# Reordering the passage between attention and experts in a one-core AdaLN block, two gate products first

## The reference

```python
mod = (silu(c) @ wmod).reshape(B, 6, 1, -1)
sa, ca, ga, sb, cb, gb = (mod[:, k] for k in range(6))
ga, gb = sign(ga) * max(|ga|, 0.25), sign(gb) * max(|gb|, 0.25)

h = layernorm(x) * (1 + ca) + sa                 # first half: linear attention, 16 heads of 16
Q, K, V = fm(h @ Wq.T + bq), fm(h @ Wk.T + bk), h @ Wv.T + bv      # fm(t) = elu(t) + 1
KV, Ksum = sum over tokens of K x V per head, sum over tokens of K
out = (Q @ KV) / (Q . Ksum + 1e-6)
x = x + ga * (out @ Wo.T + bo)

h = layernorm(x) * (1 + cb) + sb                 # second half: 8 experts, top 2
logits = cosine(h, centroids) + h @ w_route.T
g = softmax over the two largest logits
x = x + gb * sum_e g_e * (gelu(h @ w1[e] + b1[e]) @ w2[e] + b2[e])
```

## Time and profile before

| | us |
|---|---|
| median of 3 runs (376.76 to 378.42) | 376.76 |
| the profiled execution | 376.92 |
| its span, first to last instruction | 375.2 |
| PE busy, DVE busy | 350.4 (93%), 289.2 (77%) |
| POOL busy, ACT busy | 280.3 (75%), 231.3 (62%) |
| mean granted TensorE clock, share of full | 0.982 |
| DMA moved | 31.68 MB, 84 GB/s |

### The profile page before, as it was taken

How to read it: one execution, slowest core, us unless ns; L and a number is a source line. 1 busy time by engine, 2 the same in 40 slices (tenths; PEclk the granted TensorE clock), 3 DMA queues, 4 the chain that set the end, 5 groups by cost and what they waited for, 6 DMA issues and landing times.

```text
span 375.2 us, 9187 instructions
## 1 busy us (share of the span) xinstructions
PE 350.4 (93%) x2762; PEld 326.4 (87%) x2762; DVE 289.2 (77%) x820; ACT 231.3 (62%) x504; POOL 280.3 (75%) x388
## 2 busy tenths in 40 slices
PE   7999999999988474999999999999999999999895
PEld 6877888888867363999999999999999999999895
DVE  3778777778877797797797787877977977966753
ACT  4385878787745225685674764855756756756541
POOL 3457999999786739789789888888888798677200
PEclk9999999999999958999999999999999999999999
DMA  7943620000000030312214224214214223233221
GB/s 265 331 138 100 209 59 0 0 0 2 1 2 0 2 113 2 114 58 86 100 65 120 85 63 134 85 57 140 78 63 129 73 80 118 83 86 129 85 71 56
DMA packets 23704, 31.68 MB, mean 84 GB/s; under 512 B 2288, under 2 KB 14204, under 8 KB 23680
## 3 DMA queue, kind: packets, MB, share of 16 engines
q1 hardware_dynamic: 23240, 31.34, 26.6%
q10 hardware_dynamic: 440, 0.04, 0.1%
HBM read 27.04 MB, written 4.34 MB: 84 GB/s over the span
## 4 chain that ended last, share of the span: by engine, by line
PE 59%; POOL 7%; DVE 5%; issue 4%; ACT 1%; POOLq 0%; DVEq 0%
PE bank L741 18%; PE bank L743 17%; PE bank L742 17%; PE bank L749 3%; PE bank L917 2%; POOL x_sb L411 1%; PE bank L956 1%; POOL k_sum L404 1%; POOL tr_lo L394 1%; POOL early L441 1%; POOL early L451 1%; POOL rstd L378 1%; PE bank L874 1%; DVE den L1240 1%; DVE early L1213 0%
## 5 line engine op out<-in xcount | busy, mean ns | idle before, releaser
L690 ACT ACTIVATE bank<-bank,cols_sb 128x256 f32<-128x256 f32 x128 | 51.4, 439 | 46.5 <-PE bank L743 46.4
L478 POOL TENSOR_TENSOR hid_pair<-hid_g,hid_pair 128x512 fp32r<-128x512 f32 x56 | 72.5, 1294 | 7.0 <-ACT hid_pair L697 4.6
L741 PE MATMUL bank<-tr_hi,w_hi 128*128 128x256 f32 x256 | 74.2, 290 | 0.0
L743 PE MATMUL bank<-tr_hi,w_lo 128*128 128x256 f32 x256 | 72.6, 283 | 0.0
L742 PE MATMUL bank<-tr_lo,w_hi 128*128 128x256 f32 x256 | 72.4, 283 | 0.0
L741 PE MATMUL bank<-w_hi,hid_pair 128*128 128x256 f32 x252 | 70.2, 278 | 0.0
L743 PE MATMUL bank<-w_hi,hid_pair 128*128 128x256 f32 x252 | 70.1, 278 | 0.0
L742 PE MATMUL bank<-w_lo,hid_pair 128*128 128x256 f32 x252 | 70.1, 278 | 0.0
L697 ACT ACTIVATE hid_pair<-hid_g 128x512 fp32r<-128x512 f32 x64 | 40.4, 632 | 28.7 <-DVE hid_g L1298 27.4
L741 PEld LDWEIGHTS bank<-tr_hi,w_hi 128*128 128x128 f32 x256 | 48.9, 191 | 0.2
L742 PEld LDWEIGHTS bank<-tr_lo,w_hi 128*128 128x128 f32 x256 | 48.9, 191 | 0.1
(11 more groups left out here) (154 smaller groups left out, 916.7 us busy)
## 6 DMA issues: line engine op xcount, KB each, us to landing
g_bc<-g_dram SPq DMA_DIRECT2D x64, 256.0 KB, 3.5
x_sb<-in_x SPq DMA_DIRECT2D x16, 256.0 KB, 3.0
out<-x_sb SPq DMA_DIRECT2D x15, 256.0 KB, 2.3
early<-in_wmod SPq DMA_DIRECT2D x3, 512.0 KB, 7.0
q_sb<-in_w SPq DMA_DIRECT2D x2, 512.0 KB, 6.3
q_sb<-in_w SPq DMA_DIRECT2D x1, 1024.0 KB, 9.4
mod_row<-mod_dram SPq DMA_DIRECT2D x1, 1024.0 KB, 6.0
q_sb<-in_wqkvT SPq DMA_DIRECT2D x2, 384.0 KB, 5.4
```

The lines of the kernel that those rows point to most:

```text
L478: gp.tensor_tensor(hid_lo[:, p, :, :], hid_g[:, p % 2, :, :], hid_hi[:, p, :, :].bitcast(F32), ALU.subtract).then_inc(e_hlo, 1)
L690: last = ac.activation(half, half, ACT.Gelu, bias=b1_sb[:, e:e + 1])
L741: te.matmul(out_ap, l_hi, r_hi, start=start, stop=False, skip_group_check=shared)
L743: return te.matmul(out_ap, l_lo, r_hi, start=False, stop=stop, skip_group_check=shared)
```

## The change

It moves work about in the passage and leaves what is computed as it is.

- Units 13, 14 and 15 (`cast_at_end`): ScalarE makes `tr_hi` (`cast_activations`) and the expert weights' `w_hi` (`cast_weights`) in steps 12 to 14, on semaphores of their own; VectorE only subtracts.
- TensorE: `first(0, 0)` in front of `tp_o(2)`, then `first(0, 1)` to `first(0, 3)` in a row, all in step_e(-1). ScalarE does unit 0's four `gelu` there, between its other pieces.
- `mask_kv` is cut in two. `keep_ksum(1)` stays in step_e(-1); `mask_kv(1)` goes to the end of VectorE's step 0, `make_m(1)` (now in bank 7) in TensorE's step 1 behind `tp_e(3)`, `split_m(1)` to the end of VectorE's step 1. `attend` waits for it from unit 5 on, `normalise_e` (bank 7) from unit 4 on.
- VectorE: `gate(0, 0)` and `gate(0, 1)` at the head of step 0, in front of `gates_a(1)`. `denominators(3)` goes behind `modulate_e(1)`.
- GpSimd: `norm_e(0)` in front of `make_qz(2)`; `make_prod(3)` behind `exp_gates(0)`; `add_bo` of units 12 and 13 at the end of step 0, of units 14 and 15 at the end of step 1.

The diff, cut to its core:

```diff
@@ GpSimd @@
-                wait(pool, a_hi, u.count(1, 1))
+                if cast_at_end(u):
+                    wait(pool, a_hi_end, u.count(1, 1) - (NU - 3))
+                else:
+                    wait(pool, a_hi, u.count(1, 1))
...
                     exp_gates(u.plus(1))
+                if u.nth(-1):
+                    make_prod(u.plus(4))
...
-                if u.nth(-1):
-                    for j in (3, 2, 1):
-                        add_bo(unit(NU - j))
+                if u.nth(0) or u.nth(1):
+                    for j in range(2):
+                        add_bo(unit(NU - 4 + 2 * u.count(1, 0) + j))
...
+            norm_e(u0)
             make_qz(unit(2))
-            make_prod(unit(3))
-            add_bo(unit(NU - 4))
-            norm_e(u0)
@@ ScalarE @@
+            def cast_activations(u):
+                wait(act, a_hf, u.count(1, 1))
+                wait(act, a_v, u.count(1, -1))
+                ac.activation(tr_hi[:, u.h, :, :], tr_f[:, u.h, :, :], ACT.Copy).then_inc(a_hi_end, 1)
+            def cast_weights(u):
+                i = u.count(1, 0)
+                act.wait_ge(d_w, 48)
+                ac.activation(w_hi[:, i, :], w_raw[:, i, :], ACT.Copy).then_inc(w_hi_end, 1)
...
                     modulate(u.plus(1), u.plus(1).batch())
+                if u.plus(1) and cast_at_end(u.plus(1)):
+                    cast_activations(u.plus(1))
...
                     keep_v(u)
+                if u.plus(1) and cast_at_end(u.plus(1)):
+                    cast_weights(u.plus(1))
...
+                if of_later_units(u, 4):
+                    act.wait_ge(f_m_read, B)
...
+                if u.nth(-1):
+                    gelu(u.plus(1), 0)
                 if u.plus(3):
                     hi_o(u.plus(3))
...
+                if u.nth(-1):
+                    gelu(u.plus(1), 1)
                 if u.plus(2):
                     normalise_e(u.plus(2))
+                if u.nth(-1):
+                    gelu(u.plus(1), 2)
+                    gelu(u.plus(1), 3)
@@ TensorE @@
+                if of_later_units(u, 5):
+                    pe.wait_ge(f_ready, B)
                 wait(pe, o_lo, u.count(1, 1))
...
-                if u.nth(0) and p == 2:
-                    pe.wait_ge(f_m_read, B)
+                if u.nth(0) and p == 3:
+                    pe.wait_ge(f_ksrow, B)
...
-                    pe.wait_ge(f_ready, B)
                     pe.wait_ge(b2_ready, 3)
...
+                if u.nth(-1):
+                    first(u.plus(1), 0)
                 if u.plus(3):
                     tp_o(u.plus(3))
...
                 if u.nth(-1):
-                    first(u.plus(1), 0)
+                    for p in range(1, NP):
+                        first(u.plus(1), p)
...
-                if u.nth(-1):
-                    make_m(1, bank[4])
-                    first(u.plus(1), 1)
-                if u:
+                if u and not u.nth(0):
                     first(u, 2)
...
                     tp_e(u.plus(2))
+                if u.nth(1):
+                    make_m(1, bank[7])
@@ VectorE @@
             def step_e(u):
+                if u.nth(0):
+                    gate(u, 0)
+                    gate(u, 1)
                 if u.plus(1):
                     gates_a(u.plus(1))
-                if u.plus(4):
+                if u.nth(-1):
+                    keep_ksum(1, bank[5][:, 0:E])
+                if u.plus(4) and not u.nth(-1):
                     denominators(u.plus(4))
...
-                if u.nth(-1):
-                    mask_kv(1, bank[5][:, 0:E])
...
                     modulate_e(u.plus(2))
+                if u.nth(-1):
+                    denominators(u.plus(4))
                 if u.plus(3):
                     add_attention(u.plus(3))
-                if u.nth(-1):
-                    split_m(1, bank[4])
...
                     lo_e(u.plus(2))
+                if u.nth(0):
+                    mask_kv(1)
+                if u.nth(1):
+                    split_m(1, bank[7])
```

More of the change, by code:

```diff
@@ L211, in adaln_block @@
         b2_split = sem("b2_split"); b2_ready = sem("b2_ready")
-        w_hi_done = sem("w_hi_done"); w_ready = sem("w_ready")
+        w_hi_done = sem("w_hi_done"); w_hi_end = sem("w_hi_end"); w_ready = sem("w_ready")
         a_bo = sem("a_bo")
@@ L216, in adaln_block @@
         a_st = sem("a_st"); a_eps = sem("a_eps"); a_stats = sem("a_stats"); a_pow = sem("a_pow"); a_rstd = sem("a_rstd")
-        a_xn = sem("a_xn"); a_tp = sem("a_tp"); a_hf = sem("a_hf"); a_hi = sem("a_hi"); a_lo = sem("a_lo")
+        a_xn = sem("a_xn"); a_tp = sem("a_tp"); a_hf = sem("a_hf"); a_hi = sem("a_hi"); a_hi_end = sem("a_hi_end"); a_lo = sem("a_lo")
         a_qk = sem("a_qk"); a_v = sem("a_v"); a_exp = sem("a_exp"); a_vs = sem("a_vs"); a_neg = sem("a_neg")
@@ L258, in sums, with cast_at_end, of_later_units @@
             return bank[7 * t][:, 0:E] if u.nth(NU - 1) else bank[6][:, t * E:(t + 1) * E]
+        def cast_at_end(u):
+            return any(u.nth(NU - j) for j in (1, 2, 3))
+        def of_later_units(u, i):
+            return not any(u.nth(j) for j in range(i))
         def kv_bank(u):
@@ L1171, in split_weights @@
                 hi = w_hi[:, bass.ds(i, 1), :]
-                ve.tensor_copy(hi, src).then_inc(w_hi_done, 1)
-                wait(dve, w_hi_done, u.count(1, 1))
+                if cast_at_end(u):
+                    wait(dve, w_hi_end, u.count(1, 1) - (NU - 3))
+                else:
+                    ve.tensor_copy(hi, src).then_inc(w_hi_done, 1)
+                    wait(dve, w_hi_done, u.count(1, 1))
                 TT(w_lo[:, bass.ds(i, 1), :], src, hi.bitcast(F32), ALU.subtract).then_inc(w_ready, 1)
@@ L1180, in step_a @@
                     split_weights(u)
-                if u.plus(1):
+                if u.plus(1) and not cast_at_end(u.plus(1)):
                     split_a(u.plus(1))
@@ L1200, in _, with keep_ksum, mask_kv @@
             pipeline(ve, step_a, 2, 4, NU - 4, NU - 3)
-            def mask_kv(b, sums):
+            def keep_ksum(b, sums):
                 dve.wait_ge(f_ksum, b + 1)
                 ve.tensor_copy(ksum_row[:, b, :], sums).then_inc(f_ksrow, 1)
+            def mask_kv(b):
                 dve.wait_ge(f_ksrow, b + 1)
@@ L1408, in step_e @@
                     lo_e(u.plus(2))
+                if u.nth(0):
+                    mask_kv(1)
+                if u.nth(1):
+                    split_m(1, bank[7])
             dve.wait_ge(mod_got, 16)
             ve.memset(kv_m[:, :, :], 0.0)
-            mask_kv(0, bank[0][:, 0:E])
+            keep_ksum(0, bank[0][:, 0:E])
+            mask_kv(0)
             step_a(unit(NU - 3))
```

## The result

| | before | changed |
|---|---|---|
| median, first measurement (8 executions each) | 377.79 us | 373.81 us |
| lowest to highest | 376.76 to 378.97 | 373.41 to 376.31 |
| ratio, 95% interval | | 0.9913 [0.9892, 0.9933] |
| median, measured again (experiment 9) | 377.86 us | 375.60 us |
| ratio, 95% interval | | 0.9935 [0.9913, 0.9957] |

The change makes the kernel faster by 0.65 to 0.9% by the ratios, which is 2.5 to 3.3 us; the medians differ by 4.0 and 2.3. I had forecast 5.0, and a time of 371.8; the range of 369.8 to 375.0 holds the first median and not the second.

What follows compares the result with a forecast made beforehand. The passage was taken as a chain of VectorE work, with TensorE's backlog setting the end after it. Step 1 6.5 us earlier, - 1.0 - 0.8 + 0.3 = 5.0, gave 371.8 us from 376.76; range 369.8 to 375.0.

Steps and rivals of the forecast that it cites:

- The table load and g_bc: ScalarE's second table load hidden under first(0,0), else 1.3 us later; g_bc delays the gate products 0 to 0.5, taken 0.
- the rival of a late chain: Table load behind gelu's wait, g_bc landing late and blocking VectorE, some half clock: 374.0 us; chance 0.11.
- the one in which half clock lasts into step 1: Slower: TensorE's clock falls at 133.2 and stays at half in steps 0 and 1, up to some 383 us; chance 0.06.
- the signs of being wrong: VectorE idle before gate(0,0), late table load, second(0,3) or attend(5) waiting over 1 us for GpSimd, half-clock step 1, late route(2).
- Casts of units 13 to 15: Before the passage: moving these casts to ScalarE gains between 0 and 1.03 us, taken 0.7.
- second(0,0) with 14 matmuls at half clock 3.1: TensorE, step 0 behind tp_e(2): this block takes 3.1 us at half clock, with route(2) ending at 151.2.
- Here the two products in front cost their whole 1.2 us: VectorE, head of step 0: gate(0,0) and gate(0,1) delay unit 1's gates and attend(3) by 1.2 us.
- Taken 0.8: Steps behind the passage: loss from add_bo on GpSimd and VectorE's added work, bounds 0 and 2.5 us, taken 0.8.
- The +0.3 in my sum: Steady step before: about 0.3 us of stall it held, counted again, so added back to the gain.
- The rival in which GpSimd is late next: GpSimd's 2.5 us lag in steps 0 and 1 falls on TensorE nearly whole: 373.5 us; chance 0.17.
- the one without a gain: Holes only move: VectorE's chain carries 1.2 us more, ScalarE's casts take back 0.7, two rivals added: 376.2 us; chance 0.09.
- TensorE's new waits in attend are met long before: TensorE, attend from unit 5 on: the new waits are already met and cost nothing.

Runs made afterwards that it cites:

- experiment 9: The changed kernel unaltered, measured again against the kernel before: median 375.60 us, ratio 0.9935.
- Experiment 3: Changed kernel with add_bo of units 12 to 15 moved into GpSimd's idle holes: median 372.30 us, ratio 0.9843 to the kernel before.
- experiment 5: Changed kernel with add_bo in GpSimd's holes and mask_kv(1) cut short (units 8 to 15 wrong): 371.91 us, ratio 0.9861 to the kernel before.
- experiment 11: Changed kernel with add_bo in GpSimd's holes and both new waits out of the loop: 373.38 us, ratio 0.9876 to the kernel before.
- experiment 12: Changed kernel with add_bo in GpSimd's holes, TensorE's wait out of the loop, extra matmuls around tp_e(0): 372.07 us, ratio 0.9833 to the kernel before.
- experiment 7: Changed kernel with the casts of units 13 to 15 back on VectorE: 375.62 us, ratio 0.9940 to the kernel before.
- experiment 1: Changed kernel with TensorE's wait in attend and ScalarE's in normalise_e out of the loop: 374.94 us, ratio 0.9919 to the kernel before.
- experiment 10: Changed kernel with 6 and 11 more matmuls around tp_e(0), filling TensorE's holes: 373.97 us, ratio 0.9912 to the kernel before.
- Experiment 6: Changed kernel with gate(0,0) and gate(0,1) back in their steady places in step 0: 376.28 us, ratio 0.9955 to the kernel before.
- experiment 4: Changed kernel with mask_kv(1) cut short (units 8 to 15 wrong), add_bo not moved: 375.64 us, ratio 0.9934 to the kernel before.
- experiment 2: Changed kernel with only TensorE's wait in attend out of the loop, ScalarE's kept: 374.55 us, ratio 0.9912 to the kernel before.
- experiment 8: Changed kernel with 30 more matmuls filling TensorE's hole in front of attend(3): 376.01 us, ratio 0.9941 to the kernel before.

## Why the prediction was right, and where not

**The direction and the chain held.** Step -1 and step 0 are plain work of VectorE in written order: from the end of route(0) to the end of add_attention(3) I had 20.0 us (125.7 to 145.7), measured 19.6 (124.72 to 144.30). The hole in front of attend(3) was forecast at 3.9 with half clock behind it, and is 3.71 with half clock. The table load and g_bc were hidden as said. With that the rival of a late chain did not occur, nor the one in which half clock lasts into step 1: it ended at 143.8, and step 1 began at 148.4. The start of gate(0,0), 135.37, and the end of route(2), near 148.6, came before the times that I had named as signs. Of the signs of being wrong one appeared in part: attend(5) waited 1.30 us, about half of it behind add_bo (0.58 to 0.75 are left in experiments 3, 5, 11 and 12).

**Casts of units 13 to 15: 0.7 was too low, 1.3 by experiment 7.** As far as I had followed the path it was right: counted from `kv` of unit 9, z(0) moved by 0.1 and make_qz(0) by 0.6. What I left out comes behind it: VectorE's w_lo of unit 15, in front of the add_attention that tp_o(1) waits for, took 0.41 instead of 1.17 us.

**"second(0,0) with 14 matmuls at half clock 3.1" failed.** In this profile the clock was back at full during the wait for add_attention(3), and tp_e(2) to route(2) took 3.9 us instead of 5.3. With the casts (0.5 above my 0.7 at route(0)), the 0.4 of the chain and the earlier start of the first half (0.46) that is the 2.8 to 2.9 by which step 1 started sooner than forecast. It was the luck of this execution in part: in the profiles of experiments 1, 3, 10 and 12 half clock lasted beyond tp_e(2), which took 1.09 instead of 0.63, and the second interval was 13.50 to 14.54 instead of 13.42.

**"Here the two products in front cost their whole 1.2 us" failed.** Experiment 6 says the opposite. I had priced them against a VectorE that is never idle, while my own row of times had route(1) over at 137.3, 0.7 behind the end of the work in front. They cost 0.36 there and saved more behind.

**"Taken 0.8" for GpSimd and VectorE behind the passage was the large error.** The four waits are 3.46 us. Experiment 3 takes 2.25 out by moving add_bo alone, and 2.0 to 2.1 by the cleaner comparison; make_m(1), from its start to that of second(1,0), is 0.73, against 1.0. Of the 4.88 given back these two leave 0.7 to 0.8, in which TensorE is busy longer; that is not taken apart. The +0.3 in my sum, for stall in the steady step before, has no row behind it: TensorE was idle for 0.00 us in step 1 and 0.13 in step 2. The rival in which GpSimd is late next was thus the right mechanism, with about its price of 2.5. Two things made it dearer than my hand count. Step 1 started 2.9 us earlier, so mask_kv(1) was no longer under the wait for route(2), as I had said of an early TensorE but at 0.5. And mask_kv(1) took 2.95 instead of 2.3, and split_m(1) 2.83, near the 2.9 of my dearer case, not 1.9: its m_lo took 1.66, beside a make_prod that GpSimd had begun 0.43 us before it. In the kernel before the same m_lo began first, and took 0.69:

```profile
140.14 0.69 DVE L1233 TENSOR_TENSOR m_lo<-early,m_hi 128x512 fp32r<-128x512 f32 x1
```

The first of experiments 4 and 5 shows that both engines were late at once: what one saved, the other kept. (Of the rivals, the one without a gain adds up to 376.4 by its parts of 1.7, 2.2 and 0.7, not 376.2, and the 1.2 it names was in the forecast already.)

**"TensorE's new waits in attend are met long before" was true, and its price of nothing was wrong:** 0.11 us a step, 1.1 in all, by experiments 1 and 2.

So: +2.4 in the passage and +0.46 from the start of the first half, -3.4 behind it (4.88 given back up to step 3, where I had 1.5), -1.1 in the loop: 5.0 became 3.4 between the two profiles. That the first median lies in the range is in part luck: two errors of opposite sign, +2.9 and -4.5, nearly offset each other. The clock's rival had its share after all. The fall near 125, in unit 0's four blocks, which I had put at full clock, costs 1.0 to 1.4 where it comes. The one profile of the second measurement has it; whether its lower gain comes of that is not shown, as its other executions have no profile.

What stays read from the two timelines and was not tried by itself is the largest part of the gain: mask_kv(1), make_m(1) and split_m(1) taken out of step -1, and first(0,0) to first(0,3) in a row. Experiments 6 and 7 take back the smaller parts only.

## What to carry to other kernels

A gain in a passage is paid out only as far as the next engines can follow: work that is moved out of a starved stretch lands in steps where GpSimd had 1.9 us of slack, and has to be laid into an engine's measured holes, not behind its last instruction. When a piece is put in front of a chain, price it against the idle time of that engine at that place. And keep one-time waits out of loops on the engine that sets the end: order the one-time event behind something that the loop waits for anyway.

## What the runs showed of the hardware

- A wait of TensorE on a semaphore long raised, between two blocks of matmuls in a loop, costs 0.11 us a step; ScalarE's, which has slack, nothing.
- TensorE's clock fell near 125 us in eight of eleven profiles though from 105 us on no idle time before it was longer than 1.50 us. In front of attend(3), wherever a hole of 2.95 to 3.96 us was left, it was at half when the hole ended. But the hole does not always come first: in experiment 12 the clock fell at 136.1 and the hole began at 138.7.
- A subtraction of VectorE with two inputs in SBUF, 128x512, took 0.69 us when it began before GpSimd's 128x512 product and 1.66 when that was already under way.
- Filling one hole with idle matmuls moved the fall to the next (experiment 8), and the time did not fall.
